# Fused attention and mixture-of-experts block: fewer weight splits inside the attention loop, one per routed tile, and part of the causal mask added by VectorE

## The reference, cut to what matters

```
mod = silu(c) @ wmod                     # six rows a sequence: sa, ca, ga, sb, cb, gb
h = layernorm(x) * (1 + ca) + sa
q, k, v = heads(h @ Wqkv.T + bqkv)       # 16 heads of 16 channels
scores = where(causal, -inf, q k.T / 4)  # causal: keys above the diagonal
x = x + ga * (softmax(scores) v @ Wout.T + bout)
h = layernorm(x) * (1 + cb) + sb
logits = h @ router_w.T                  # 8 experts, top 1, weight sigmoid(top)
routed = (up * silu(gate)) @ down[e]     # gate, up = (h * weight) @ gate_up[e], 512 wide
shared = (silu(h @ sg) * (h @ su)) @ sd
x = x + gb * (shared + routed)
```

## Time and profile before

| what | value |
|---|---|
| median of three runs | 447.87 us |
| the profiled execution | 447.57 us |
| its span, first to last instruction | 445.8 us |
| mean granted TensorE clock | 0.991 |
| attention loop with exponentials | about 49 to 262 us |
| between the loop and the routed tiles | about 262 to 320 us |
| routed tiles | about 320 to 438 us |

### The profile page before, as it was taken

How to read it: one execution, slowest core, us unless ns; L and a number is a source line. 1 busy time by engine, 2 the same in 40 slices (tenths; PEclk the granted TensorE clock), 3 DMA queues, 4 the chain that set the end, 5 groups by cost and what they waited for, 6 DMA issues and landing times.

```text
span 445.8 us, 8579 instructions
## 1 busy us (share of the span) xinstructions
PE 394.8 (89%) x3009; PEld 225.2 (51%) x3009; DVE 312.9 (70%) x631; ACT 230.9 (52%) x412; POOL 209.3 (47%) x254
## 2 busy tenths in 40 slices
PE   3889989799899899889989889999898899999991
PEld 3344534346454455444443545746555566666660
DVE  7798596499888788999687758899735543444441
ACT  2646558786758656557657563544335233323320
POOL 4756937452269624872336731006104445545242
PEclk9999999999999999999999999999989999999997
DMA  8655595448604795312255154636454244433210
GB/s 270 195 160 111 176 250 143 159 126 245 170 36 131 175 260 151 97 49 85 96 167 166 49 182 150 202 129 197 140 183 102 54 89 85 74 84 65 27 21 0
DMA packets 42448, 58.52 MB, mean 131 GB/s; under 512 B 5092, under 2 KB 33380, under 8 KB 42408
## 3 DMA queue, kind: packets, MB, share of 16 engines
q1 hardware_dynamic: 28616, 32.02, 25.5%
q10 hardware_dynamic: 8640, 17.83, 12.6%
q0 software_dynamic: 5152, 8.14, 9.0%
HBM read 38.42 MB, written 20.46 MB: 132 GB/s over the span
## 4 chain that ended last, share of the span: by engine, by line
PE 57%; DVE 23%; ACT 7%; issue 6%; POOL 5%; ACTq 1%; DVEq 0%; POOLq 0%
PE bank L1562 35%; DVE mx L1189 5%; PE bank L1718 4%; PE bank L1702 4%; PE bank L1673 3%; DVE W L1290 3%; PE bank L1942 2%; ACT W L923 2%; PE bank L1650 1%; ACT W L888 1%; DVE x_sb L1234 1%; POOL W L779 1%; DVE st L1129 1%; DVE rowg L1290 1%; PE bank L1675 1%
## 5 line engine op out<-in xcount | busy, mean ns | idle before, releaser
L923 ACT ACTIVATE W<-bank 128x512 f32<-128x512 f32 (+1 forms) x176 | 93.5, 561 | 53.8 <-PE bank L1702 37.7
L1189 DVE TENSOR_REDUCE mx<-bank 128x1 f32<-128x384 f32 (+3 forms) x176 | 104.3, 631 | 21.1 <-PE bank L1675 18.1
L1562 PE MATMUL bank<-W 128*128 128x256 f16 (+2 forms) x756 | 102.1, 286 | 6.0 <-DVE x_sb L1234 2.2
L1562 PEld LDWEIGHTS bank<-W 128*128 128x128 f16 x756 | 71.9, 98 | 36.6 <-issue 6.6
L779 POOL TENSOR_SCALAR_AFFINE_SELECT W<-W 128x512 f32<-128x512 f32 x64 | 45.1, 706 | 78.5 <-ACT W L923 78.4
L1562 PE MATMUL bank<-W,h2T 128*128 x276 | 68.6, 386 | 1.8 <-issue 1.6
L856 POOL DMA_INDIRECT out<-h2T,sidx x23 | 36.7, 1594 | 70.3 <-DVE h2T L1528 70.0
L1702 PE MATMUL bank<-W 128*128 128x512 f16 (+3 forms) x256 | 62.6, 301 | 5.2 <-ACT W L923 4.3
L1673 PE MATMUL bank<-W 126*128 126x128 f16 (+3 forms) x208 | 51.9, 300 | 4.5 <-DVE mx L1189 3.6
L1718 PE MATMUL bank<-W 128*32 128x128 f32 (+3 forms) x512 | 47.5, 444 | 3.6 <-POOL W L779 3.6
L1562 PE MATMUL bank<-h2T,W 128*128 128x512 f16 x192 | 43.1, 379 | 0.6 <-DVE W L1305 0.6
(11 more groups left out here) (176 smaller groups left out, 568.6 us busy)
## 6 DMA issues: line engine op xcount, KB each, us to landing
stage<-in_gup ACTq DMA_DIRECT2D x14, 512.0 KB
qk_d<-W SPq DMA_DIRECT2D x48, 128.0 KB
W<-qk_d SPq DMA_DIRECT2D x32, 192.0 KB, 4.6
w_d<-rowg ACTq DMA_DIRECT2D x9, 512.0 KB, 3.1
W<-w_d SPq DMA_DIRECT2D x9, 512.0 KB, 6.1
stage<-in_down ACTq DMA_DIRECT2D x7, 512.0 KB
x_sb<-in_x SPq DMA_DIRECT2D x4, 512.0 KB, 9.3
h_d<-gbb SPq DMA_DIRECT2D x4, 512.0 KB, 5.4
```

Of the source, the lines that this page charges most:

```text
L923: a.activation(PT[j][:, i:i + m, :], t_bank(N)[:, 0:m * w].rearrange("p (i n) -> p i n", i=m), ACT.Exp).then_inc(s_exp, 1)
L1189: v.tensor_reduce(mx_v[:, b % 2, hp0 // 4, par, i:i + m, t], s_bank(N)[:, 0:m * w].rearrange("p (i n) -> p i n", i=m), AX.X, ALU.max).then ...
L1562: i = t_.matmul(outp, l, r, start=(n == 0), stop=(n == len(prods) - 1), **kw)
```

## The change

Three things change.

1. **Fewer units in the attention loop.** `DIRECT` goes from 18 to 15: batch 1 splits 3 weight units where it split 4, batch 3 splits 4 where it split 6. Four units are split between loop and routed tiles, as before. `ORDER` puts expert 7 last, so that four routed experts (4, 3, 5, 7) are split late in place of three.
2. **Late units, one a routed tile.** Where tiles 0 to 3 took units 22 to 26, with two of them at the last, tiles 0 to 7 take units 19 to 26, one each. On VectorE a tile's `split_low` comes after its hidden product and not before. TensorE waits for the two gate and up units of an expert before the gate half of tile r, and for its down unit before `down_rows`.
3. **Mask of single-head units.** For units with one head, from `LAG` on, TensorE's mask matmul is left out; `maxima` becomes one `tensor_tensor_reduce`, which adds `maskw` (128 x 512 bfloat16, zero but for its last 128 columns) to the bank, writes the sum back into the bank, and takes the maximum.

```diff
-ORDER = [0, 2, 1, E, 7, 6, 4, 3, 5]
+ORDER = [0, 2, 1, E, 6, 4, 3, 5, 7]
 BOUNCED = 9
-DIRECT = BOUNCED + 9
+DIRECT = BOUNCED + 6
...
-          1: {8: 4, 19: 5, 30: 6, 41: 7},
-          2: {8: 8, 18: 9, 28: 10, 38: 11},
-          3: {4: 12, 10: 13, 16: 14, 22: 15, 28: 16, 34: 17}}
-LATE_HIGHS = {0: [22], 1: [23], 2: [24], 3: [25, 26]}
-LATE_LOWS = {1: [22], 2: [23], 3: [24], 4: [25, 26]}
-LATE_MOVES = {0: [20, 21], 1: [22], 2: [23]}
+          1: {14: 4, 28: 5, 41: 6},
+          2: {8: 7, 18: 8, 28: 9, 38: 10},
+          3: {4: 11, 14: 12, 24: 13, 34: 14}}
+LATE = {r: DIRECT + 4 + r for r in range(3 * (E + 1) - DIRECT - 4)}
...
-        maskb = sb("maskb", [P, P], BF16)
+        maskw = sb("maskw", [P, S], BF16)
+        maskb = maskw[:, S - P:S]
...
-                link(g.memset(maskb[:, :], 0.0))
+                link(g.memset(maskw[:, :], 0.0))
...
-                elif k == BOUNCED + 6:
+                elif k == BOUNCED + 3:
                     ac.wait_ge(s_pv, 16 * (B - 1))
... (ScalarE, tile r)
-                for k in LATE_MOVES.get(r, []):
-                    move_halves(k)
-                for k in LATE_HIGHS.get(r, []):
-                    split_high(k)
+                if r == 0:
+                    move_halves(DIRECT + 2)
+                    move_halves(DIRECT + 3)
+                elif r - 1 in LATE:
+                    move_halves(LATE[r - 1])
+                if r in LATE:
+                    split_high(LATE[r])
... (VectorE, maxima)
-                v.tensor_reduce(mx_v[:, b % 2, hp0 // 4, par, i:i + m, t],
-                                s_bank(N)[:, 0:m * w].rearrange("p (i n) -> p i n", i=m),
-                                AX.X, ALU.max).then_inc(s_mx, 1)
+                if m > 1 or N < LAG:
+                    v.tensor_reduce(mx_v[:, b % 2, hp0 // 4, par, i:i + m, t],
+                                    s_bank(N)[:, 0:m * w].rearrange("p (i n) -> p i n", i=m),
+                                    AX.X, ALU.max).then_inc(s_mx, 1)
+                else:
+                    v.tensor_tensor_reduce(s_bank(N)[:, 0:w], s_bank(N)[:, 0:w], maskw[:, S - w:S], 1.0, NEG,
+                                           ALU.add, ALU.max,
+                                           mx_v[:, b % 2, hp0 // 4, par, i:i + m, t]).then_inc(s_mx, 1)
... (VectorE, tile r)
-                for k in LATE_LOWS.get(r, []):
-                    split_low(k)
                 if r < RT:
...
                     v.scalar_tensor_tensor(hid[:, r % 2], [S1, M1][r % 2][:, :], 1.0 / WS,
                                            g32[:, r % 2], ALU.mult, ALU.mult).then_inc(s_rhid, 1)
+                if r in LATE:
+                    split_low(LATE[r])
... (TensorE, scores)
-                    t_.matmul(bk[:, w * i:w * (i + 1)], qs[r][0:P - 2, hp, par, P * t:w],
-                              ks[r][0:P - 2, hp, 0:w], start=(i == 0), stop=False, skip_group_check=True)
-                t_.matmul(bk[:, 0:m * w].rearrange("p (i n) -> p i n", i=m)[:, :, w - P:w], identb[:, :],
-                          maskb[:, :].unsqueeze(1).to_broadcast([P, m, P]), start=False, stop=True,
-                          skip_group_check=True).then_inc(s_s1, 1)
+                    q = t_.matmul(bk[:, w * i:w * (i + 1)], qs[r][0:P - 2, hp, par, P * t:w],
+                                  ks[r][0:P - 2, hp, 0:w], start=(i == 0), stop=(m == 1), skip_group_check=True)
+                if m > 1:
+                    q = t_.matmul(bk[:, 0:m * w].rearrange("p (i n) -> p i n", i=m)[:, :, w - P:w], identb[:, :],
+                                  maskb.unsqueeze(1).to_broadcast([P, m, P]), start=False, stop=True,
+                                  skip_group_check=True)
+                q.then_inc(s_s1, 1)
... (TensorE, down_rows)
+                if r in ORDER[DIRECT // 3:]:
+
+                    pe.wait_ge(*low_done(3 * ORDER.index(r) + 2))
... (TensorE, before the gate half of tile r)
-                        pe.wait_ge(*low_done(3 * ORDER.index(r) + 2))
+                        pe.wait_ge(*low_done(3 * ORDER.index(r) + 1))
```

More of the change, by code:

```diff
@@ L683, in mask_constants @@
                 link(g.tensor_copy(identb[:, :], ident[:, :]))
-                link(g.memset(maskb[:, :], 0.0))
-                g.affine_select(out=maskb[:, :], in_=maskb[:, :], compare_op=ALU.is_ge, fill=NEG,
+                link(g.memset(maskw[:, :], 0.0))
+                g.affine_select(out=maskb, in_=maskb, compare_op=ALU.is_ge, fill=NEG,
                                 base=0, pattern=[[-1, P]], channel_multiplier=1).then_inc(s_const, 1)
@@ L1642, in scores_apart @@
                         w = P * (t + 1)
-                        t_.matmul(s_bank(N)[:, w * (i + 1) - P:w * (i + 1)], identb[:, :], maskb[:, :],
+                        t_.matmul(s_bank(N)[:, w * (i + 1) - P:w * (i + 1)], identb[:, :], maskb,
                                   start=(left[N] == m), stop=False, skip_group_check=True)
```

## The result

The changed kernel takes 441.3 us, the median of four runs (440.56 to 441.82), against 447.73 us for the kernel before beside it; the ratio is 0.9859, with a 95% interval of 0.9824 to 0.9895. That is 6.4 us less (4.7 to 7.9 us by the interval), where 8.9 were forecast for the median: 439 us, in a range of 434.5 to 446.5. The direction is right, and the measured time is inside the range. It is also inside the likeliest case's own range (435.5 to 442.5), but that is partly luck: the terms of the sum were off in both directions.

What follows compares the result with a forecast made beforehand. No engine was taken as full in the attention loop, where TensorE and VectorE take turns; TensorE bounds the later routed tiles. Terms -4.1 (routed tiles), -2.0 (batch 3), -0.6 (batch 1), -2.3 (mask) sum to -9.0: 439 us, range 434.5 to 446.5.

Steps and rivals of the forecast that it cites:

- the likeliest case: Whole kernel: the forecast itself, 439 us with its own range of 435.5 to 442.5, chance 0.60.
- routed tiles, -4.1: Routed tiles: low halves hide behind the hidden product, -4.55 us, less 0.5 us of new waiting at tile 7.
- without a late unit the three tiles would take: Routed tiles 2 to 4: 14.13 us at 4.71 each in place of 18.68, so 4.55 us can be had.
- Tile 7: Routed tile 7: TensorE waits before the gate half for unit 25's split, 0.5 us, between 0 and 1.2.
- the mask, -2.3: Attention loop: mask matmuls leaving TensorE gain 1.2 us in the first stretch, 1.1 in the second, nothing in the third.
- 2.0 us I take 60%: First loop stretch: of 2.0 us of TensorE mask time, 60% reaches the path, -1.2 us, as banks hand over between engines.
- batch 3, -2.0: Attention loop, 208 to 264 us: two units fewer shorten ScalarE's waits; half of 3.9 us gained, range 0 to -4.
- two thirds, 3.9 us, should go with them: Batch 3: of ScalarE's three waits for low halves, 5.8 us together, 3.9 us should vanish with two units.
- batch 1, -0.6: Attention loop, batch 1: one unit fewer gains 0.6 us, by halving some 1.2 us of VectorE.
- the one with the mask matmul hidden anyway: Attention loop: mask matmul already hidden, batch stalls partly so; 442.5 us, chance 0.08.
- the result with an instruction of its own: Loop maxima: a second VectorE instruction reads out each maximum, 0.167 us for each of 104; 444 us, chance 0.16.
- VectorE as a new bound: Attention loop: dearer maxima make VectorE the bound; 453 us at 0.30 us more each, near 491 at two passes; chance 0.11.

Runs made afterwards that it cites:

- the kernel that removes it: Changed kernel with five, not four, weight units split between loop and routed tiles, the rest in tiles 0 to 6: 440.01 us, 0.9823 to the kernel before.
- late order alone: Kernel before with only its own late units 22 to 26 put one a tile in tiles 0 to 4, behind the hidden product: 443.07 us, ratio 0.9906.
- parts 1 and 2: Changed kernel with all masks added by TensorE as before and maxima by the plain reduction: 441.15 us, 0.9858 to the kernel before.

## Why the prediction was right, and where it was off

**Right: routed tiles, -4.1.** The step "without a late unit the three tiles would take" 4.71 us each held: tiles 2 to 4 take 14.01 us in the trace, 4.67 less than before, where the term was -4.55, and the place behind the hidden product hides the low half. Two things are off. Tile 7 was undersized: 0.5 forecast, 1.05 us in the trace (1.6 us by the kernel that removes it, with an error as large). I had priced the end of the low half and not enough of what comes behind the wait, 0.9 us from the low half's end to the first matmul. And tile 1, which before had a low half too, isn't in the sum: it took 6.52 us at half clock and now takes 4.62. The prediction had this only as a clock that might be at half speed again, 1.8 us either way. The late order alone measured -4.2, near the term, with tile 1 in it and without the wait of tile 7.

**Wrong: the mask, -2.3.** Measured 0 alone (0.9995) and 0 with the other parts (0.9858 against 0.9859). VectorE's price, 3.1 to 4.8 us against 4.2, was as forecast, so the size of the new operation was not what failed. The step that failed is "2.0 us I take 60%": TensorE's time is worth far less on the path of the loop. Up to the 89th exponential, where no half clock interferes, the 64 mask matmuls are 3.8 us of TensorE by the prediction's 0.06 each; the loop gets 1.1 us shorter without them and without any price to VectorE, and about 0.5 us with the change's masks. Behind that, up to 2 us may have gone with the clock, which is not shown.

**Wrong: batch 3, -2.0.** "two thirds, 3.9 us, should go with them": they didn't, since a wait belongs to the place at which a unit is moved and not to the number of units. Three waits of 6.0 us were left, one of them at a new place. Measured: nothing.

**Too small: batch 1, -0.6.** Measured 1.9 us in the traces. I halved the duration of a low half; at the place shown, what it costs is the chain behind it in VectorE's queue.

**The sum.** The parts as measured are -4.2 for the late order, -1.9 for batch 1, 1.05 for tile 7 and nothing for batch 3 and the mask: -5.1 us, where -6.4 were measured (4.7 to 7.9 by the interval). The 1.3 us between them are within the errors and have no cause here; the late order alone had a lower mean clock than parts 1 and 2 (0.988 against 0.991), which may be a part of it.

**Of the rivals**, the one with the mask matmul hidden anyway (442.5) describes part 3 best. Of the result with an instruction of its own the mechanism came and the price did not. The trace has the 104 reads, and my "one instruction is issued" was wrong; but an operation with its read costs 0.03 to 0.05 us of VectorE's busy time over the reduction (3.1 to 4.8 us over 104), and not 0.167, since the read overlaps its neighbours. So the third stretch has 48.99 us of VectorE and not 53.8, and the 444 us did not come. The Trainium skill's rule on such operations (VectorE: DVE Perf Modes, Two Vector instructions with no wait between them), two instructions where the accumulator is written out, agrees with the 104 reads of these rows. VectorE as a new bound did not come either; its time at two passes, "near 491", should have read 493. The half clock at tile 1 stands in both traces with the old order of late units and in none of the eleven with the new one, and others came up in the loop. That the new order prevents it is not shown: the idle times ahead of it are still there, and some runs of the kernel before have a mean clock of 0.995 and 0.996, as high as traces without any such stretch.

## What to carry to other kernels

Put work that only has to be done by some time behind the product that the busiest engine waits for, not ahead of it, and look at what hole each engine has there; the price of a piece in an in-order queue is what stands behind it, and a wait moves with its place rather than going with its cause. Time taken from an engine that is 90% busy is worth little while it waits for others in turn: price it by a run that leaves the work out and puts nothing in its place (here 1.1 of 3.8 us). Compare traces in stretches with the same granted clock. A last weight that a tile needs wants to be ready a tile early, as the read of an offset stands behind the wait.

## What the runs showed of the hardware

- An add, a write back to the PSUM bank and a maximum in one VectorE instruction over 512 columns took 700 ns, a plain maximum 681; over 384 columns 568 and 544. A read of 138 ns follows each and overlaps its neighbours: both together are 0.03 to 0.05 us of VectorE's busy time over the plain maximum (four pairs of kernels, 104 operations each).
- From the end of the split that TensorE waited for to its first matmul with an address read from memory behind that wait: 0.9 us (0.9 to 1.0 in six traces).
- Stretches of some 3.4 us at half clock came at like places in several kernels (around 30, 186 and 245 us), and were missing in others of the same program up to there. TensorE had been idle only 0.64 us ahead of the first and 1.5 to 2.1 us ahead of the last, and the same idle times stand at full clock in other traces (0.64 us at 26.7 us in the kernel with parts 1 and 2, 2.11 at 243.7).
- What one costs: with one around 30 us the loop starts about 1 us later (51.8 to 52.0 against 50.5 to 50.9), and the tile in which it fell took 6.52 us where 4.62 is the time at full clock.
